# Two heads side by side in the TensorE array: head stacks of 96 rows become two tiles of 64 rows in a decoder's attention loops

## The reference

```
scores = einsum('bnqh,bnkh->bnqk', q, k) / sqrt(16)     # causal mask in the self attention only
out    = einsum(softmax(scores), v)                     # 512 queries, 512 or 1601 keys
```

## Time and profile before

| | |
|---|---|
| runs before | 1757.94, 1761.57, 1765.12 us; median 1761.57 us |
| the profiled execution | span 1755.5 us from first to last instruction |
| mean granted TensorE clock | 0.931 |
| busy in the span | TensorE matmul 88%, VectorE 63%, ScalarE 45%, GpSimd 17% |
| queries and keys of sa prepared | 690 to 763 us |
| sa loop | 763 to 943.5 us |
| t3 | 943.5 to 1004 us |
| xa loop | 1004 to 1651 us |

### The profile page before, as it was taken

How to read it: one execution, slowest core, us unless ns; L and a number is a source line. 1 busy time by engine, 2 the same in 40 slices (tenths; PEclk the granted TensorE clock), 3 DMA queues, 4 the chain that set the end, 5 groups by cost and what they waited for, 6 DMA issues and landing times. The chain is left out here.

```text
span 1755.5 us, 28756 instructions
## 1 busy us (share of the span) xinstructions
PE 1545.8 (88%) x8850; PEld 841.1 (48%) x8850; DVE 1107.1 (63%) x2286; ACT 791.1 (45%) x1566; POOL 304.7 (17%) x323
## 2 busy tenths in 40 slices
PE   6776689987999979759899699999999999999876
PEld 3444357873599966424445323333333323332355
DVE  4778515553122217957775699887878878886256
ACT  2333214431111101336664327776767767777522
POOL 3555500003000016710002420000000000000141
PEclk9987789998999989979999869998999989999998
DMA  9544410003599942763334612222232222220001
GB/s 338 162 133 139 139 30 1 1 10 111 177 328 334 330 143 79 251 192 98 96 97 112 199 29 57 57 57 58 60 92 65 68 58 57 57 57 1 1 1 48
DMA packets 178018, 189.77 MB, mean 108 GB/s; under 512 B 12171, under 2 KB 157231, under 8 KB 177906
## 3 DMA queue, kind: packets, MB, share of 16 engines
q1 hardware_dynamic: 170092, 172.14, 32.6%
q0 software_dynamic: 4080, 12.33, 1.9%
q10 hardware_dynamic: 3734, 3.83, 0.7%
HBM read 129.65 MB, written 58.34 MB: 107 GB/s over the span
## 5 line engine op out<-in xcount | busy, mean ns | idle before, releaser
L1772 DVE TENSOR_REDUCE xa_part<-psum 128x1 f32<-128x401 f32 (+1 forms) x1024 | 512.4, 567 | 91.2 <-PE psum L1646 85.6
L1747 ACT ACTIVATE xa_P<-psum 128x512 f32<-128x512 f32 (+1 forms) x832 | 434.2, 600 | 160.9 <-PE psum L1671 160.9
L1646 PE MATMUL psum<-xa_K,sa_Q 96*128 96x401 bf16 (+1 forms) x1024 | 328.1, 353 | 9.8 <-PEq L1809 9.4
L1671 PE MATMUL psum<-sa_Q,xa_K 98*128 98x512 bf16 (+1 forms) x832 | 319.4, 390 | 14.4 <-issue 7.7
L1684 PE MATMUL psum<-xa_P,xa_V 128*32 128x512 f32 (+1 forms) x1664 | 226.3, 616 | 0.1
L1671 PEld LDWEIGHTS psum<-sa_Q,xa_K 98*128 98x128 bf16 (+1 forms) x832 | 81.8, 100 | 271.8 <-ACT xa_P L1747 192.7
L1646 PEld LDWEIGHTS psum<-xa_K,sa_Q 96*128 96x128 bf16 x1024 | 102.6, 100 | 102.8 <-DVE xa_part L1772 33.1
L1772 DVE TENSOR_REDUCE sa_part<-psum 128x1 f32<-128x128 f32 (+3 forms) x256 | 113.7, 487 | 59.0 <-PE psum L1649 57.8
L1747 ACT ACTIVATE sa_P<-psum 128x512 f32<-128x512 f32 (+3 forms) x256 | 101.1, 440 | 54.3 <-PE psum L1674 51.6
L118 POOL TENSOR_TENSOR x_sb<-x_sb,x_bo_sb 128x256 f32<-128x256 f32 x16 | 11.6, 750 | 632.4 <-SPq L1809 632.4
L1239 PE MATMUL psum<-xtT,wgu 128*128 128x128 f32 x992 | 115.9, 275 | 1.6 <-ACT xtT L1275 1.6
(11 more groups left out here) (221 smaller groups left out, 2226.4 us busy)
## 6 DMA issues: line engine op xcount, KB each, us to landing
wgu<-in_f_gu SPq DMA_DIRECT2D x31, 1024.0 KB, 7.5
xa_K<-kx SPq DMA_DIRECT2D x96, 200.1 KB, 4.5
wdn<-in_f_dn SPq DMA_DIRECT2D x31, 512.0 KB, 7.7
vx<-xv_v SPq DMA_DIRECT2D x48, 256.0 KB, 3.2
xa_V<-vx SPq DMA_DIRECT2D x16, 768.0 KB
sa_Q<-qs SPq DMA_DIRECT2D x16, 384.0 KB, 3.7
sa_K<-ks SPq DMA_DIRECT2D x16, 384.0 KB, 4.6
sa_Q<-qx SPq DMA_DIRECT2D x16, 384.0 KB, 3.8
```

Of the source, the lines that this page charges most:

```text
L1646: last = pe.matmul(o, Qst[0:QK_ROWS, u, h, qt * P:(qt + 1) * P], Kst[0:QK_ROWS, u, h, k0:k1], start=True, stop=not causal)
L1671: last = pe.matmul(o[0:r, 0:w_], Kst[0:ONE + 2, u, h, kt * P:kt * P + r], Qst[0:ONE + 2, u, h, q0(kt):L], start=True, stop=not causal)
L1747: act.activation(Pr[0:r, (u * KT + kt) % R, h, 0:w_], ring2(1 + u * S1 + pos(g, n))[0:r, 0:w_], ACT.Exp, scale=SCALE).then_inc(s_exp, 1)
L1772: dve.tensor_reduce(part[:, h * TB + qt, e:e + 1], ring1(n)[:, 0:k1 - k0], AX, ALU.max).then_inc(s_1free, 1)
```

## The change

The six products become two halves of three: `K_PARTS` ((0,1,0),(2,1,0)) and `Q_PARTS` ((0,0,1),(0,1,2)). A half has 48 rows (`HALF`). Even heads have their rows in partitions 0 to 47, odd heads in 64 to 111 (`base`), and the two heads' matmuls name the 64-row tile of the array in which they run (`tile_position`).

- The maximum pass uses the first half alone (three products), and one unit is now two heads: two matmuls of 48 rows into two banks, and one VectorE maximum over both. 32 units a group in xa, 8 in sa; `ring1` has two places of two banks.
- A step of the score pass is two heads: four matmuls, half 0 (50 rows with the maxima rows) and half 1 (48 rows) of each head, accumulated. The wait on `ring2` is once for the pair, for the bank of the second head.
- A mask matmul of 128 rows becomes four of 64 rows for two heads; the constants for it are copied into `cbx` by four DMAs at the start of the cross attention of layer 0.
- DMAs: Q loads 1 to 4 a group, K loads 1 to 4 (sa) and 6 to 12 (xa), maxima rows 2 to 4; a K block of sa is stored by 5 DMAs and not 3.
- The ones become blocks of 32 rows, two memsets for each of three buffers: for sa on GpSimd in layer 0's last stage, for xa on VectorE in the first three steps of t3, with SyncE's K loads waiting for them.
- The order: the `LEAD` of units is 4 (pairs), the step of the fold `M_STEP` is 43 instead of 42 in xa and 9 in both for sa.

```
-    units = [(h, qt, e) for h in range(G) for qt in range(TB) for e in range(CUTS)]
+    units = [(h, qt, e) for h in range(0, G, 2) for qt in range(TB) for e in range(CUTS)]
-    R1 = 4
+    R1 = 2
...
-        ring1 = lambda n: PS[:, n % R1 * BANK:(n % R1 + 1) * BANK]
+        ring1 = lambda n: PS[:, n % R1 * 2 * BANK:(n % R1 + 1) * 2 * BANK].rearrange("p (j n) -> p j n", j=2)
...
                     h, qt, e = units[n]
                     k0, k1 = keys_of(qt, e)
-                    o = ring1(n)[:, 0:k1 - k0]
-                    last = pe.matmul(o, Qst[0:QK_ROWS, u, h, qt * P:(qt + 1) * P], Kst[0:QK_ROWS, u, h, k0:k1],
-                                     start=True, stop=not causal)
+                    for j in range(2):
+                        at, to = base(j), place(h, 0)
+                        last = pe.matmul(ring1(n)[:, j, 0:k1 - k0], Qst[at:at + HALF, u, to, qt * P:(qt + 1) * P],
+                                         Kst[at:at + HALF, u, to, k0:k1], start=True, stop=not causal, tile_position=(at, 0))
                     if causal:
-                        last = pe.matmul(o[:, k1 - P:k1], env.identb, env.mask_q, start=False, stop=True)
+                        last = hide(lambda j: ring1(n)[:, j, k1 - P:k1], P)
...
+                def scores(g, u, kt, h, first):
                     n = kt * G + h
                     if n == 0:
-                        pe.wait_ge(s_ones, R)
-                        pe.wait_ge(s_mq[u], 32 * (first + 1))
-                    bank_free(g, pos(g, n))
+                        pe.wait_ge(s_mq[u], 64 * (first + 1))
+                    bank_free(g, pos(g, n + 1))
...
+                    for half in range(2):
+                        for j in range(2):
+                            at, to, depth = base(j), place(h, half), HALF + 2 * (half == 0)
+                            last = pe.matmul(out(j), Kst[at:at + depth, u, to, kt * P:kt * P + r],
+                                             Qst[at:at + depth, u, to, q0(kt):L], start=(half == 0),
+                                             stop=(half == 1 and not causal), tile_position=(at, 0))
+                            if half == 1 and not causal:
+                                last.then_inc(s_2, 1)
                     if causal:
-                        last = pe.matmul(o[0:r, 0:P], env.identb, env.mask_k, start=False, stop=True)
-                    last.then_inc(s_2, 1)
+                        hide(lambda j: out(j)[:, 0:P], 2 * P).then_inc(s_2, 2)
...
-                        dve.tensor_reduce(part[:, h * TB + qt, e:e + 1], ring1(n)[:, 0:k1 - k0], AX, ALU.max).then_inc(s_1free, 1)
+                        dve.tensor_reduce(part[:, h // 2 * TB + qt:COLS:COLS // 2, e], ring1(n)[:, :, 0:k1 - k0], AX,
+                                          ALU.max).then_inc(s_1free, 1)
...
                 for c in range(STEPS):
+                    if queries and c < hb.RING:
+                        hb.ones(dve, c).then_inc(s_ones, 1)
```

More of the change, by code:

```diff
@@ L239, in __init__ @@
         self.width_of = width_of or (lambda n: width)
-        self.slots, self.per = slots, len(slot_runs(slots(0)))
+        self.slots = slots
+        self.per = lambda n: sum(len(slot_runs(run)) for run in slots(n))
         sb, sem = env.alloc(c)
@@ L263, in act_hi @@
         if n >= self.ring:
-            act.wait_ge(self.s_out[u], 16 * self.per * (n // self.ring))
+            act.wait_ge(self.s_out[u], 16 * self.per(n) * (n // self.ring))
         if self.rope:
@@ L765, in _ @@
             def _(sp):
+                for tile in range(2):
+                    for half in range(2):
+                        sp.dma_start(env.cbx[tile * ROW_TILE:(tile + 1) * ROW_TILE, half, :],
+                                     env.cb[half * ROW_TILE:(half + 1) * ROW_TILE, :]).then_inc(s_cbx, 16)
                 full = (CT - 1) * P
@@ L1093, in _ @@
                 def _(pool):
+                    for u in range(hb.RING):
+                        hb.ones(pool, u)
                     pool.wait_ge(s_slot, 1)
@@ L1510, in semaphores, with ones @@
         self.s_q = [sem(f"{name}_q{u}") for u in range(self.RING)]
+    def ones(self, engine, u):
+        for tile in range(2):
+            end = (tile + 1) * ROW_TILE
+            last = engine.memset(self.K[end - 32:end, u, 0:G // 2, :].rearrange("p h n -> p (h n)"), 1.0)
+        return last
     def load_q(self, sp, g, u):
-        sp.dma_start(self.Q[0:QK_ROWS, u, :, :], self.qp(g)).then_inc(self.s_q[u], 16)
+        for half in range(2):
+            for odd in range(2):
+                at, to = base(odd), place(0, half)
+                sp.dma_start(self.Q[at:at + HALF, u, to:to + G // 2, :], self.qp(g, half)[:, odd:G:2, :]).then_inc(self.s_q[u], 16)
     def load_k(self, sp, g, u):
-        if self.causal:
-            sp.dma_start(self.K[0:QK_ROWS, u, :, :], self.kp(g)).then_inc(self.s_k[u], 16)
-        else:
-            for j, part in enumerate(K_PARTS):
-                sp.dma_start(self.K[j:QK_ROWS:len(K_PARTS), u, :, :], self.kp(g, part)).then_inc(self.s_k[u], 16)
+        for half in range(2):
+            for odd in range(2):
+                at, to = base(odd), place(0, half)
+                if self.causal:
+                    sp.dma_start(self.K[at:at + HALF, u, to:to + G // 2, :],
+                                 self.kp(g, half)[:, odd:G:2, :]).then_inc(self.s_k[u], 16)
+                else:
+                    for j, part in enumerate(K_PARTS[half]):
+                        sp.dma_start(self.K[at + j:at + HALF:PROD, u, to:to + G // 2, :],
+                                     self.kp(g, part)[:, odd:G:2, :]).then_inc(self.s_k[u], 16)
 def heads_loop(nc, env, name, hb, OT, stored=None):
@@ L1627, in _, with hide @@
                         reload(g, g % R)
-            @block.gpsimd
-            def _(pool):
-                for u in range(R):
-                    pool.memset(Kst[ONE:ONE + 2, u, :, :].rearrange("p h n -> p (h n)"), 1.0).then_inc(s_ones, 1)
             @block.tensor
             def _(pe):
+                def hide(out, mask):
+                    for half in range(2):
+                        for j in range(2):
+                            at = base(j)
+                            last = pe.matmul(out(j), env.cbx[at:at + ROW_TILE, half, 0:P],
+                                             env.cbx[at:at + ROW_TILE, half, mask:mask + P],
+                                             start=False, stop=(half == 1), tile_position=(at, 0))
+                    return last
                 def unit(g, u, n, first):
@@ L1660, in bank_free @@
                         pe.wait_ge(s_exp, g * S1 + (p - 1))
-                def score(g, u, kt, h, first):
+                def scores(g, u, kt, h, first):
                     n = kt * G + h
                     if n == 0:
-                        pe.wait_ge(s_ones, R)
-                        pe.wait_ge(s_mq[u], 32 * (first + 1))
-                    bank_free(g, pos(g, n))
-                    o = ring2(1 + u * S1 + pos(g, n))
+                        pe.wait_ge(s_mq[u], 64 * (first + 1))
+                    bank_free(g, pos(g, n + 1))
                     r = rows(kt)
                     w_ = L - q0(kt)
-                    last = pe.matmul(o[0:r, 0:w_], Kst[0:ONE + 2, u, h, kt * P:kt * P + r], Qst[0:ONE + 2, u, h, q0(kt):L],
-                                     start=True, stop=not causal)
+                    out = lambda j: ring2(1 + u * S1 + pos(g, n + j))[0:r, 0:w_]
+                    for half in range(2):
+                        for j in range(2):
+                            at, to, depth = base(j), place(h, half), HALF + 2 * (half == 0)
[4 more added lines that the diff above has]
+                                last.then_inc(s_2, 1)
                     if causal:
-                        last = pe.matmul(o[0:r, 0:P], env.identb, env.mask_k, start=False, stop=True)
-                    last.then_inc(s_2, 1)
+                        hide(lambda j: out(j)[:, 0:P], 2 * P).then_inc(s_2, 2)
                 def values(g, u, kt, first):
@@ L1699, in group @@
                     for kt in range(KT):
-                        for h in range(G):
-                            n = kt * G + h
-                            score(g, u, kt, h, first)
+                        for h in range(0, G, 2):
+                            n = kt * G + h + 1
+                            scores(g, u, kt, h, first)
                             while done < due[n]:
```

63 lines of the change are left out of this document (37 added, 26 removed).

## The result

The kernel after takes 1859.97 us (median of four runs, 1858.46 to 1865.69), the kernel before on the same chip 1761.01 us: ratio 1.0573, 95% interval 1.054 to 1.0605. The profiled execution has a span of 1858.2 us against 1755.5, so 102.7 us to account for.

A forecast was written before the change was run, and what follows sets the result against it. TensorE was taken as the bound. xa +45, sa +24, the stage before sa +11 and t3 +17 make +97 us on the 1755.5 us span; with 6.1 us for the median about 1859 us, range 1785 to 1915.

The forecast's parts named there:

- xa, +45: Cross attention loop: longer rounds +43 us in 15 groups, last group +5, before the first group -3; +45 us in all.
- The round of 3.07: In xa: 1.33 us from pair A to B plus 1.74 from B to next A, against 2.85 before.
- a pair adds 401 columns: VectorE in xa: a pair's maximum takes 0.93 us, so 2.3 us a round instead of 2.5.
- the prelude: Before xa's first group: 64 maxima of 32.3 us become 32 pairs of 29.8 us, -3 us.
- falls half into the idle gap: xa's round: half of TensorE's stream saving, 0.47 us in all, lands where it idles behind pair A, worth nothing.
- sa, +24: The sa loop: each of 16 groups takes 1.5 us more (0.9 to 2.0), +24 us, ends +5 and +40.
- Rival 4: Gaps in TensorE's work lower its clock, priced on xa's steady stream: +50 us on top, 1910 us; chance 0.06.
- The stage before sa, +11: SyncE's queue sets this stage's end; more stores and 18 more loads cost +11 us, ends 4 and 15.
- t3, +17: Stage t3: six VectorE memsets of 2.7 to 3.4 us and 9 extra query loads, +17 us, ends 8 and 22.
- 1: Rival: the two row tiles don't overlap, xa's round is 3.93 us, about 2080 us in all; chance 0.08.
- 2: Rival: the loops stay about even and only the stages pay, xa +10, sa +5, 1795 us; chance 0.14.
- 3: Rival: faster, xa's round goes by the stream alone at 2.38 us, xa -95 us, 1690 us; chance 0.12.

The follow-up runs named there:

- combined kernel: Kernel after with values split in halves, ones as 4-byte words and sa's first loads on ScalarE: 1783.86 us; with loops written out 1777.70 us.
- edits of order: Kernel before with the score's wait once for two heads and VectorE taking two heads' maxima at once: 1828.27 us, ratio 1.0377.

## Why the prediction was right

The sum was +97 us on the profiled span, measured +102.7; the median 1859 against 1859.97. That the medians agree to 1 us is luck. The span was forecast 5.7 us too short, and the 6.1 us added for the median came out at 1.8 (1859.97 against a span of 1858.2), 4.3 too much; the profiled execution of the kernel before happened to be the shortest of its runs, that of the kernel after lay at its median. The size of the terms is the fairer test. Point by point:

- **xa, +45, measured +55** (+52.6 with the tail, which became 2 us shorter). The round of 3.07 was put together from 1.33 and 1.74; it is 1.29 and 1.71 with two units, so the round trip and the first head's 0.64 us were right. What was undersized is the term of the units: I counted VectorE's pairs as 2.3 us a round, hence free, and priced no wait. Rounds with three pairs take 3.15, a group averages 3.11 a round. The step that failed is "a pair adds 401 columns" as a pure saving: put into the kernel before by itself, it costs 11 us in xa. The last group (2.46 to 2.89 us a round, from exponentials that start at 1726.72 and 1729.61; forecast 2.86) and the prelude (-2) came as forecast.
- **The reason.** That the lost look-ahead costs the time was shown: put into the kernel before by itself it makes 49 us. But my account of it, that a pair waits for its second head's bank, was only half of it. Waits for each head change nothing; the fourth head's bank and the first head's longer way to its exponential give the same round. And the saving of the tiles does not vanish whole, as "falls half into the idle gap" already said: 1.2 us are left in a group of 40.4 without a branch.
- **sa, +24, measured +23.2, but from other parts.** The period rose by 1.05 us and not 1.5 (15.8 us in 15). The rest is the last group: from the last fold to t3 20.4 us instead of 13.3. Most of that goes with the clock, which was granted at half there: with a wait for each head it stayed at 1.00 and the stretch took 15.8 us, though that kernel's order differs too. Rival 4 put the clock on xa, where nothing of it shows (0.96), and gave no place to this.
- **The stage before sa, +11, measured +6.8.** SyncE's queue does set the end, with loads of 0.45 to 0.58 us each and stores of 0.46 to 0.68: the eight more small stores and 18 more loads add 3.0 and 6.7 us to its issues, 9.7 in all, but the other stores in between take 5.0 us less than before, more than I had allowed. The size is not good to better than the 6 us by which sa's first fold moves between executions.
- **t3, +17, measured +20.1.** Memsets are 2.73 us long, as the lower bound had it, but with a pause of 0.70 us before each they take 3.43 apiece, the upper end, 20.6 us for six. That they cost what they take was shown by halving them (-10 us). The clock is granted at half for the first 8 us and at 0.67 to 0.71 for 28 more; what that costs in a stretch where TensorE mostly waits for VectorE, no run shows.
- **Rivals.** 1 fell: 0.45 us for a pair's four products, where four one after the other take 4 x 0.215 = 0.86. The factor of two that the prediction quoted stands in the Trainium skill, TensorEngine Tiling (Array Packing), under Theoretical Speedup in the section Overview and not in Tiling Modes; this trace comes near it (1.9). 2 and 3 fell: the round is not near 2.85 or 2.38. The point made against 3, that the round trip can't hide in the units, held with both orders of issue.
- **What would show it.** Twos of exponentials, TensorE idle before every second pair, a group of 40.4 us, a pair's maximum of 0.99 us: all there. VectorE's busy time in the steady part fell to 472 us.

What stays open: why the combined kernel gains so little from the loops written out, and what part of sa's +1.05 us is masks, weight loads or maxima rows. The edits of order alone give 0.65 of it (11.31 us). Against the rest, 6 us in 15 groups, stand waits that grew, 11 us for the maxima rows and 21 for ScalarE's banks, and one for K that shrank by 11; no run took them apart. Open too is why a branch costs 5 to 8 us a time in the kernels before and after and only 1 to 2 in the one with both edits of order.

## What to carry to other kernels

When a change removes work from the busiest engine, ask first what hands the next work to it: here halving the stream of the maximum pass was worth 1.2 us in a group of 40, since three banks and a longer way to the first result set the round. Count the chain from the first product of a round to the reuse of its bank, and put independent work in the hole (the split values gave back 63 us), but check that there is a hole: the same edit cost 32 us where there was none. Tiles pay only if neighbours in the queue use the same tiling, and an operation made twice as large needs a queue that is still deep enough. And compare equal stretches: a mean over groups with and without a branch hid that gain.

## What the runs showed of the hardware

- Changing between the whole array and two row tiles cost 0.10 us each way; accumulated products of two heads in two row tiles took 0.45 us for four of 512 columns, in either order of issue.
- The granted clock fell to half within sa's last group, where TensorE had no units to do and waited 0.3 to 0.9 us before most pairs, and stayed so for the first 8 us of t3. In the kernel before it was 1.00 there, in the one with a wait for each head too, and also in xa's last group of the kernel after, where TensorE waits 0.75 us before every second pair; so what made it fall is open.
- In xa of the kernel before, a branch of the hardware loop leaves TensorE idle for 2.3 to 2.9 us (7.7 in the three) without a wait that the profile shows. Behind the first of them the granted clock is 0.58 and then 0.50 for 10 us (1193 to 1203). A group takes 6 to 7 us more for it (5 to 8 in the kernel after). With the loops written out this is gone. It is not a fixed price: with the wait in pairs, or with both edits of order, the same branch costs 1.1 to 2.0 us and the clock stays at 1.00, and in sa of the kernel before it shows nowhere.
- The issue of a load of Q or K for half a group took 0.45 to 0.58 us on SyncE and 0.48 to 0.99 us on ScalarE, 0.64 in the mean.
- A VectorE memset of 3202 bf16 elements was 2.73 us long, but the next one behind it started 3.43 us after its start; with 1601 float32 elements 1.39 and 1.76 us.
